# Spreading softmax sums with four transfers inside SBUF, and splitting the normalised product over three engines

## What is computed

```python
ada = silu(c) @ W_ada + b_ada      # six vectors of modulation for each sequence
h = layernorm(x) * (1 + scale_msa) + shift_msa
q, k, v = split(h @ W_qkv + b_qkv) # 16 heads of 18 channels
o = softmax(q @ k.T * 18 ** -0.5) @ v
x = x + gate_msa * (o @ W_proj + b_proj)
h = layernorm(x) * (1 + scale_mlp) + shift_mlp
x = x + gate_mlp * (gelu(h @ W_fc1 + b_fc1) @ W_fc2 + b_fc2)
```

## Time and profile before

| what | value |
|---|---|
| runs, median (lowest to highest of 3) | 2104.65 us (2098.85 to 2105.66) |
| profiled execution, its own time | 2105.64 us |
| its span, first to last instruction | 2103.9 us |
| mean granted TensorE clock | 0.969 |
| busy share of the span: PE, DVE, ACT, POOL | 94%, 58%, 53%, 48% |
| DMA, mean of the span | 99 GB/s |

### The profile page before, as it was taken

One profiled execution on the slowest core, in us unless ns is written; L12 is line 12 of the kernel. 1 busy time (PEld: TensorE's weight loads), 2 busy tenths in 40 slices (PEclk: granted clock), 3 DMA queues, 4 the chain that ended last, 5 costly groups with the idle time before them and its releaser, 6 DMA issues. The chain is left out here.

```text
span 2103.9 us, 49860 instructions
## 1 busy us (share of the span) xinstructions
PE 1967.8 (94%) x16599; PEld 1754.2 (83%) x16599; DVE 1210.3 (58%) x2720; ACT 1120.0 (53%) x1932; POOL 1003.5 (48%) x1031
## 2 busy tenths in 40 slices
PE   4785799999999999899999999999999999999997
PEld 2553589999899988789899899998789998998986
DVE  6874466546556475556556465575565565564641
ACT  4232455564655645554655656645555656656552
POOL 1002345545455554645455454554655554554534
PEclk9797899999999999999999999999999999999998
DMA  6523443332333323432333323333433323333320
GB/s 171 139 79 118 126 117 87 100 99 80 104 89 94 99 78 105 146 106 78 108 93 90 95 84 105 97 82 101 137 89 90 98 81 106 96 90 93 86 80 26
DMA packets 138971, 207.34 MB, mean 99 GB/s; under 512 B 35700, under 2 KB 96274, under 8 KB 137822
## 3 DMA queue, kind: packets, MB, share of 16 engines
q1 hardware_dynamic: 111582, 169.78, 29.0%
q10 hardware_dynamic: 25040, 29.18, 4.9%
q0 software_dynamic: 2256, 7.17, 1.3%
HBM read 99.51 MB, written 20.82 MB: 57 GB/s over the span
## 5 line engine op out<-in xcount | busy, mean ns | idle before, releaser
L2070 DVE TENSOR_REDUCE maxima<-scores 128x4 f32<-128x1024 f32 x384 | 460.4, 1222 | 186.1 <-PE scores L1819 181.0
L1411 POOL TENSOR_TENSOR hidden<-g_full,hidden 128x512 fp32r<-128x512 f32 (+1 forms) x240 | 280.4, 1177 | 358.4 <-ACT hidden L1647 357.1
L1604 ACT ACTIVATE probs<-scores 128x1024 f32<-128x1024 f32 x384 | 383.1, 1027 | 95.4 <-PE pv_ps L1856 56.8
L1881 PE MATMUL mlp_ps<-h_mlp,w_up 128*128 128x256 f32 (+1 forms) x3024 | 410.0, 288 | 9.5 <-ACT hidden L1647 5.4
L1881 PEld LDWEIGHTS mlp_ps<-h_mlp,w_up 128*128 128x128 f32 (+1 forms) x3024 | 381.0, 190 | 40.4 <-issue 20.1
L1736 PE MATMUL mlp_ps<-w_down,hidden 128*128 128x288 f32 x2592 | 388.8, 295 | 0.0
L1736 PEld LDWEIGHTS mlp_ps<-w_down,hidden 128*128 128x128 f32 x2592 | 369.4, 188 | 18.1
L1819 PE MATMUL scores<-k_stack,q_stack 108*128 108x512 f32 x768 | 241.3, 406 | 20.8 <-DMA k_stack<-qk 18.2
L1842 PE MATMUL scores<-q_stack,k_stack 110*128 110x256 f32 x1536 | 245.7, 292 | 3.6 <-ACT probs L1604 2.4
L1842 PEld LDWEIGHTS scores<-q_stack,k_stack 110*128 110x128 f32 x1536 | 207.8, 191 | 32.5 <-issue 18.9
L1594 ACT ACTIVATE neg_max<-att_ps 16x256 fp32r<-16x256 f32 x48 | 17.9, 373 | 387.3 <-PE att_ps L1829 387.3
(11 more groups left out here) (230 smaller groups left out, 2849.6 us busy)
## 6 DMA issues: line engine op xcount, KB each, us to landing
q_stack<-qk SPq DMA_DIRECT2D x144, 180.0 KB
k_stack<-qk SPq DMA_DIRECT2D x288, 90.0 KB
inv_sum<-inv_scratch ACTq DMA_DIRECT2D x192, 128.0 KB, 2.6
k_stack<-qk SPq DMA_DIRECT2D x288, 54.0 KB
x_mid<-out_x SPq DMA_DIRECT2D x48, 288.0 KB, 4.2
out_x<-x_out SPq DMA_DIRECT2D x48, 288.0 KB, 3.1
x_in<-out_x SPq DMA_DIRECT2D x47, 288.0 KB, 3.9
q_stack<-qk SPq DMA_DIRECT2D x144, 72.0 KB
```

What stands on the lines that cost most here:

```text
L1411: tt(out, full, high.bitcast(F32), ALU.subtract).then_inc(signal, 1)
L1604: evict(probs[:, u % 4, :, :, :], scores[u % 2][:, :, :, :], ACT.Exp, scale=SCALE)\
L1881: last = mm(up_bank[n % 2][:, (m % 2) * T:(m % 2 + 1) * T], w[:, m * P:(m + 1) * P], h, start=count == 0, stop=count == 6)
L2070: nc.vector.tensor_reduce(out=maxima[:, :, :, u], in_=scores[u % 2][:, :, :, :], axis=AX.X, op=ALU.max).then_inc(s_max, 1)
```

## The change

In step 2 the one transfer to HBM becomes four transfers, each from one row of `o_full` (one partition, 4096 B) to 32 partitions x 128 B of `sums`; the load of step 3 is gone with its wait. `inverse` waits for the four. In step 5 DVE writes the full product in place in `o_full`; ACT rounds it into `o_att[0]` with two Copy activations (`high_o`, new) that stand behind the last of its transfers and its table load and ahead of `attention_modulate`; POOL has only the subtraction left.

```diff
-    dram["sum_scratch"] = nc.dram_tensor("sum_scratch", (4, 2 * 512), F32, kind="Internal").ap()
...
                 for half in range(2):
-                    pool.wait_ge(s_o, 2 * it + half + 1)
-                    tt(o_full[:, half, :], o_full[:, half, :], inv_sum[:, half, :], ALU.mult).then_inc(s_o_norm, 1)
-                for half in range(2):
-                    pool.wait_ge(s_o_norm, 2 * it + half + 1)
+                    pool.wait_ge(s_o_hi, 2 * it + half + 1)
                     low(o_att[1][:, half, :], o_full[:, half, :], o_att[0][:, half, :], s_o_lo)
...
             def gather_sums(it):
                 act.wait_ge(s_o_full, 2 * it + 2 + PRE)
-                act.dma_start(dram["sum_scratch"], o_full[HD:P:32, :, :].rearrange("i h t -> i (h t)"))\
-                   .then_inc(s_sum_st, 16)
-
-            def load_sums(it):
-                act.wait_ge(s_sum_st, 16 * it + 16)
-                act.dma_start(sums[:, :], dram["sum_scratch"].rearrange("i (j e) -> (i j) e", e=32)).then_inc(s_sum, 16)
+                for i in range(4):
+                    row = 32 * i + HD
+                    act.dma_start(sums[32 * i:32 * i + 32, :],
+                                  o_full[row:row + 1, :, :].rearrange("i h t -> i (h t)")).then_inc(s_sum, 16)
+
+            def high_o(it):
+                for half in range(2):
+                    act.wait_ge(s_o, 2 * it + half + 1)
+                    evict(o_att[0][:, half, :], o_full[:, half, :], ACT.Copy).then_inc(s_o_hi, 1)
...
                 gather_sums(it)
                 if before:
                     gelu(it - 1, 0)
-                load_sums(it)
                 if before:
                     gelu(it - 1, 1)
...
                     spread_inverse(it, range(4))
+                high_o(it)
                 if after_next:
                     attention_modulate(it + 2, (0, 1, 2), None if before else it + 2, it if before else None)
...
             def inverse(it):
-                dve.wait_ge(s_sum, 16 * it + 16)
+                dve.wait_ge(s_sum, 64 * it + 64)
                 nc.vector.reciprocal(inv_few[:, :], sums[:, :]).then_inc(s_inv, 1)
...
                 for half in range(2):
-                    tt(o_att[0][:, half, :], o_full[:, half, :], inv_sum[:, half, :], ALU.mult).then_inc(s_o, 1)
+                    tt(o_full[:, half, :], o_full[:, half, :], inv_sum[:, half, :], ALU.mult).then_inc(s_o, 1)
```

More of the change, by code:

```diff
@@ L1081, in layers @@
         s_o_full = sem("s_o_full")
-        s_sum_st = sem("s_sum_st")
         s_sum = sem("s_sum")
@@ L1087, in layers @@
         s_o = sem("s_o")
-        s_o_norm = sem("s_o_norm")
+        s_o_hi = sem("s_o_hi")
         s_o_lo = sem("s_o_lo")
```

## The result

The changed kernel takes 2237.87 us (median of 4 runs, 2236.82 to 2239.60), against 2103.40 us (2098.85 to 2105.66) for the kernel before: a ratio of 1.0643, 95% interval 1.0623 to 1.0663. The profiled execution took 2238.6 us with a span of 2236.9. The forecast was 2203 with a range of 2139 to 2242, so the time lies at the upper edge, where the prediction had put the case in which the clock falls behind half of the stalls (2240).

A forecast was written before the change was run, and what follows sets the result against it. PE was taken to bound the kernel, with ACT's two gelus on its path in 47 half steps. From 2105.6 us, +110.5 for issues, -11.4 for waits removed and -1.3 for POOL gave 2203 us, range 2139 to 2242.

The forecast's parts named there:

- What bounds the kernel: At `up(m, 2)` and `up(m, 3)`: PE bounds, and ACT's gelu 0 and gelu 1 are on its path, within 0.06 us.
- The 45 waits put down to "issue": In the list of waits: 45 short waits labelled "issue", taken as looking harmless only through labels; nine named gelu, 5.3 us.
- Four issues in place of one: On ACT ahead of gelu 0: four issues of 0.69 us replace the 0.53 us gather, +2.35 us per half step, +110.5.
- No load and no wait ahead of gelu 1: On ACT between gelu 0 and gelu 1: PE no longer waits at `up(m, 3)`, -11.4 us together.
- The copies: ACT's two rounding copies, 0.60 us each, and its wait for DVE: hidden by 3.9 us of cover, cost nothing.
- POOL's relief: POOL loses two products, 2.93 us, so its subtraction starts earlier; PE gains only in the last half step, -1.3 us.
- The likeliest case, 2203: Whole program: +110.5 - 11.4 - 1.3 on the profiled 2105.6 us gives 2203 us; chance 0.49.
- a rival with a chance of 0.17: PE's clock falls behind the new stalls: 2240 us if half of them bring a fall, 2277 if all; chance 0.17.
- A granted clock well under 0.969: Sign in PE's profile, listed among those that would show the prediction wrong.
- some 2.1 us more than before: Sign that the prediction is right: every half step takes some 2.1 us more, with PE idle at `up(m, 2)`.
- The case of the almost free issue: On ACT ahead of gelu 0: issues cost only some 0.05 us each, making the kernel faster, 2090 us; chance 0.05.
- that of ACT's new wait: ACT's wait for DVE, or the copies' order, delays PE: each further microsecond adds 47, say 2250 us; chance 0.04.

The follow-up runs named there:

- the experiment with the split alone: Kernel before, with only the product split changed (DVE full product, ACT rounds, POOL subtracts), sums still through HBM with one issue: 2097.1 us, ratio 0.9986.

## Why the prediction was right, point by point

**What bounds the kernel** held: PE, with gelu 0 on its path within 0.06 us in the rows and 0.11 in the median. The experiments that moved or added issues all follow from that one meeting of two rows. One reading beside it was wrong. The 45 waits put down to "issue" in the earlier trace rows are not these meetings under another name. They stand one product earlier, ahead of `up(m, 1)` and behind the product of the probabilities:

```profile
1012.98 1.74 PEld L1881 LDWEIGHTS mlp_ps<-h_mlp,w_up 128*128 128x128 f32 x14 [0.41 <-issue]
```

and they are still there, 46 waits and 18.9 us, in the kernels in which PE waits for neither gelu. The short meetings with the gelus don't appear in the list at all; only the starts of the weight loads show them. No term of the sum used the 18.5 us.

**Four issues in place of one** was the right mechanism, a little too large. The issues of the changed kernel, from one line of it (ns min, median, max):

```profile
L1616 ACTq DMA_DIRECT2D sums<-o_full x192: 552/624/924, 229.6 to 2185.2; - x192
```

The median is 0.62 us where I had taken 0.69 from the nearest row; by place in the group of four it is 0.56, 0.61, 0.65 and 0.76, so a later one costs more than the first; the stall grew by 2.13 us (2.24 less 0.11) and not by 2.35, and summed over the half steps by 101 us where the forecast had 110.5. Of the two rows it was between, the group of four in a row gave 2.32 for the four, the single issue with SBUF on both sides 2.88 with gaps; 2.62 to 2.70 lies in the middle.

**No load and no wait ahead of gelu 1**: 12.2 us back against 11.4 forecast. Where the clock has fallen, the first load of `up(m, 3)` stands 0.213 us behind the one before it and not 0.12; but so does every load beside it, so this is the lower clock and no wait.

**The copies** cost nothing, as forecast, with 3.8 us of cover against 3.9. **POOL's relief** is worth next to nothing, as forecast.

**The step that failed is the sum's silence on the clock.** The likeliest case, 2203, counted a stall of 2.4 us as if only the idle time were lost, and left the clock to a rival with a chance of 0.17. With the measured terms and no clock the sum is 2105.6 + 101 - 12.2 - 1.3 = 2193.1 us; the profiled execution took 2238.6. Of the 45.5 us between, 43.7 are the time by which the same weight loads took longer. The rival had the price per fall nearly right, 1.56 us, and 32 more stretches at about 1.4 us each is what came. That 2238 lies so near the rival's 2240 is in part luck: the issues cost 9.5 us less than in its sum, and the clock 7 us more. A granted clock well under 0.969 was among the signs that the prediction had named against itself, and it came: 0.947. The rival's chance had rested on two stalls of 2.37 and 3.05 us, only one of which brought the clock down, and two such rows, in a stall that comes 47 times, speak for a chance near a half.

The forecast that each half step takes "some 2.1 us more than before" matches 39.79 less 37.83 = 1.96 where the clock held; where it fell, it is 3.69. The case of the almost free issue is refuted by the row above: none of the 192 issues took less than 0.55 us. So is that of ACT's new wait, by the experiment with the split alone.

## What to carry to other kernels

Before counting what a transfer takes to land, look at what its issue stands in front of: a queue that issues and computes pays for every issue in its own order, and where the bound engine meets that queue within a tenth of a microsecond, each issue goes straight into the time. One strided transfer of 0.59 us did the work of four of 0.62, and moving it behind the gelu for which PE waits took away PE's last wait there. Another engine can take the issues over only as far as its own order has slack. And when an edit gives the bound engine a new stall, price the clock with it: here a stall of 2.24 us made a half step 2.0 us longer or 3.7, depending on whether the clock fell.

## What the runs showed of the hardware that I had not expected

The issue from SBUF to SBUF hardly grows with the number of target partitions here: 0.59 us for one transfer from 4 rows to 128 partitions, 0.56 for the first of a group from 1 row to 32. It grows with its place in a group on ACT: 0.56, 0.61, 0.65, 0.76 us in the changed kernel, and 0.58, 0.75 with two more issues. POOL issued the same shape in 0.57 us as the first and 0.50 as each later one.

```profile
L1474 POOL DMA_DIRECT2D sums<-o_full x192: 496/496/604, 225.7 to 2046.5; - x192
```

And the clock did not answer the stall in proportion: with stalls of 0.73 and 1.61 us in each half step there were as many stretches at 1.2 GHz as with 0.11, and with 2.24 us there were five times as many. Nor does the length of a single stall tell whether the clock falls behind it. In the changed kernel it fell behind 30 stalls of 2.01 to 2.33 us, and did not behind 16 others of 2.07 to 2.73. What tells them apart, I did not test.
